# Attention sums kept with heads on partitions, key 0 added by TensorE, division moved to the feed-forward stage

## What is computed

```python
x = x + attn(layernorm(x))
x = x + ffn(layernorm(x))

# attn: attend = |i - j| <= 128, or i == 0, or j == 0
weights = softmax(where(attend, q @ k.T * 0.25, -inf))
out = (weights @ v) @ Wo.T
# ffn: h = x @ ternary(w_fc).T + gate * (x @ v.T @ fast_b.T @ u.T)
#      ternary(relu(h)**2 @ w_proj)
```

## Time and profile before

| | |
|---|---|
| three timed runs | 1067.39, 1068.22, 1068.65 us; median 1068.22 |
| the profiled execution's own time | 1071.5 us |
| its span in the trace | 1068.9 us |
| TensorE busy | 1031.5 us (97%) |
| VectorE busy | 921.4 us (86%) |
| ScalarE busy | 775.2 us (73%) |
| GpSimd busy | 699.6 us (65%) |
| granted TensorE clock | 0.995 of full speed |

### The profile page before, as it was taken

One profiled execution on the slowest core, in us unless ns is written; L12 is line 12 of the kernel. 1 busy time (PEld: TensorE's weight loads), 2 busy tenths in 40 slices (PEclk: granted clock), 3 DMA queues, 4 the chain that ended last, 5 costly groups with the idle time before them and its releaser, 6 DMA issues.

```text
span 1068.9 us, 40083 instructions
## 1 busy us (share of the span) xinstructions
PE 1031.5 (97%) x16071; PEld 789.2 (74%) x16071; DVE 921.4 (86%) x3202; ACT 775.2 (73%) x1328; POOL 699.6 (65%) x945
## 2 busy tenths in 40 slices
PE   9999999799999999999999999999999999999997
PEld 8888887466665666557665666588888888888886
DVE  7889987799999999999999999487888888888885
ACT  7989987687888888887888878854566554556554
POOL 3575556688888888898888888843344443344443
PEclk9999999899999999999999999999999999999999
DMA  6999989878667766776677653512122221123001
GB/s 210 263 314 276 286 231 267 155 136 154 129 139 156 157 126 137 158 145 130 139 138 160 131 120 70 143 38 80 59 89 90 60 60 60 60 79 95 26 21 40
DMA packets 187019, 142.33 MB, mean 133 GB/s; under 512 B 61625, under 2 KB 186577, under 8 KB 186833
## 3 DMA queue, kind: packets, MB, share of 16 engines
q1 hardware_dynamic: 186832, 139.77, 55.3%
HBM read 87.98 MB, written 50.95 MB: 130 GB/s over the span
## 4 chain that ended last, share of the span: by engine, by line
PE 60%; DVE 11%; issue 4%; SPq 3%; ACT 2%; DMA 1%; POOL 0%; DVEq 0%; ACTq 0%
PE e_psum L1616 13%; PE e_psum L1638 12%; PE e_psum L1347 9%; PE e_psum L1906 6%; PE e_psum L1908 6%; DVE a_masked L1362 4%; PE e_psum L1888 3%; PE e_psum L1887 3%; DVE n_stats L144 2%; DVE f_x L2028 2%; SPq L1321 2%; PE e_psum L231 1%; PE e_psum L233 1%; PE e_psum L232 1%; PE e_psum L1892 1%
## 5 line engine op out<-in xcount | busy, mean ns | idle before, releaser
L1692 ACT ACTIVATE a_weights<-e_psum 128x1024 f32<-128x1024 f32 (+1 forms) x512 | 391.4, 809 | 85.2 <-PE e_psum L1616 84.7
L1362 DVE CUSTOM_DVE_ANT_0 a_masked<-e_psum,band 128x290 f32<-128x290 f32 (+1 forms) x992 | 387.7, 445 | 37.9 <-PE e_psum L1347 32.1
L1526 POOL TENSOR_SCALAR_AFFINE_SELECT a_weights<-a_weights 128x1024 f32<-128x1024 f32 x256 | 273.9, 1094 | 48.6 <-ACT a_weights L1692 47.2
L1950 POOL TENSOR_TENSOR f_square<-f_relu 128x512 f32<-128x512 f32 x128 | 147.6, 1154 | 212.8 <-ACT f_relu L1939 189.6
L1347 PE MATMUL e_psum<-e_k,e_q 96*32 96x290 bf16 (+2 forms) x4096 | 236.5, 287 | 15.6 <-DVE max L1362 6.5
L1616 PE MATMUL e_psum<-e_q,e_k 128*32 128x384 bf16 (+2 forms) x5632 | 241.6, 280 | 5.8 <-ACT a_weights L1692 3.6
L1638 PE MATMUL e_psum<-a_weights,a_v 128*17 128x384 f32 (+2 forms) x2816 | 221.7, 389 | 2.0 <-issue 1.4
L1616 PEld LDWEIGHTS e_psum<-e_q,e_k 128*32 128x32 bf16 x5632 | 132.0, 96 | 97.0 <-ACT a_weights L1692 40.9
L1347 PEld LDWEIGHTS e_psum<-e_k,e_q 96*32 96x32 bf16 x4096 | 116.8, 97 | 84.1 <-DVE max L1362 46.7
L1906 PE MATMUL e_psum<-w_w_t,f_square_hi 128*128 128x256 f32 x512 | 129.4, 287 | 4.6 <-DVE f_square_lo L2004 4.6
L1939 ACT ACTIVATE f_relu<-e_psum,w_mag 128x512 f32<-128x512 f32 x128 | 87.4, 683 | 54.5 <-PE e_psum L1892 54.5
(11 more groups left out here) (215 smaller groups left out, 1925.3 us busy)
## 6 DMA issues: line engine op xcount, KB each, us to landing
k_parts<-p_k_parts SPq DMA_DIRECT2D x48, 258.0 KB, 4.7
q_parts<-p_q_parts SPq DMA_DIRECT2D x48, 256.0 KB, 5.5
e_q<-q_parts SPq DMA_DIRECT2D x64, 192.0 KB, 4.0
e_k<-k_parts SPq DMA_DIRECT2D x60, 193.5 KB, 3.7
v_ones<-p_va SPq DMA_DIRECT2D x16, 544.0 KB, 5.9
p_x<-in_x SPq DMA_DIRECT2D x16, 512.0 KB, 7.0
e_q<-q_parts SPq DMA_DIRECT2D x64, 128.0 KB, 3.9
f_o<-attention SPq DMA_DIRECT2D x16, 512.0 KB, 4.7
```

The source lines that it names most:

```text
L1362: dve.tensor_tensor_reduce(out=masked[:, place + lo:place + hi], in0=bank[:, lo:hi], in1=self.band[:, lo:hi], scale=1.0, scalar=NEG, op0=A ...
L1526: pool.affine_select(out=blocks, in_=blocks, compare_op=ALU.is_ge, fill=0.0, base=0, pattern=[[0, NQ // 2 * HEAD_COLS // P // CUT_STEP], [ ...
L1692: act.activation(pe_w[:, us.upar, lo:hi], score[c % 2][:], ACT.Exp).then_inc(s_exp, 1)
L1950: pool.tensor_tensor(sh.r2[:, j % 4, :], sh.r[:, j % 4, :], sh.r[:, j % 4, :], ALU.mult).then_inc(self.s_sq, 1)
```

## The change

What it does, part by part:

- **Sums.** VectorE copies the sums out of PSUM as they are, heads on partitions (`dve_sums_copied`), and SyncE stores each unit's 128 rows of 512 float32 in DRAM, now laid out as [group, head, channel or denominator, token]. The transposition, the reciprocal and four of GpSimd's operations in each unit are gone.
- **Key 0.** ScalarE's weights `p0` of two units are turned by VectorE (128 by 32 elements, once in two units), brought by a DMA onto one partition of each head's quarter (`p0_row`), and TensorE adds them: four matmuls in each unit (`key0_sums`), one for each head, with one contraction row, 17 columns of weights and 512 moving columns, all float32. They start the accumulation, so they come ahead of the blocks. Head j takes row 32j of the array and columns 32j on. The value row of key 0 is kept on every partition. The gate that excludes key 0 for queries whose window has it is now an addition ahead of the exponential.
- **Shift.** The two copies of the split in three move from ScalarE to GpSimd.
- **TensorE's order.** `AFTER_TILE` is written anew, and `BEFORE_TILES` is empty.
- **Division.** In unit 50's step the denominators of the first three sequences are loaded as a tile of 128 by 768, VectorE takes one reciprocal over it in the next step, and it is stored again; the last sequence's 128 by 256 follow in the feed-forward stage (step of group 5). For each group, 16 heads' factors are then loaded and repeated over 16 partitions each, and GpSimd multiplies them into the loaded sums, two operations of 128 by 512 a group (`pool_combine`).
- **Feed-forward.** As channels already stand on partitions, `pe_turn_o` is gone; the split reads SBUF, one group earlier than before. The first half of `pe_attention` moves to where the transpositions were, the second stays behind `pe_output` of the sixth part. The last sum of unit 63 is done in two pairs of heads, as before, now with two key 0 matmuls ahead of each pair.

The diff, cut to its core:

```diff
-P0_BUFS = 2 * UPG
+P0_BUFS = UPG
+SUM_BUFS = 3
...
+ROW0_STORED, FACTORS, COMBINED = 9, 50, (55, UNITS - 2, UNITS - 1)
+LAST_DEN = 4
...
-BEFORE_TILES = (("score", 0), ("score", 1))
+BEFORE_TILES = ()
 AFTER_TILE = (
-    (), (("score", 2),), (), (), (("score", 3), ("score", 4), ("score", 5)),
-    (), (), (("sum", 0),), (("score", 6), ("score", 7), ("sum", 1)),
...
+    (), (), (("score", 0), ("score", 1)), (("score", 2),), (), (("key0", 0), ("score", 3), ("score", 4)), (),
+    (), (), (("score", 5), ("sum", 0)), (("score", 6), ("score", 7)), (), (("sum", 1),),
...
+    def dve_factor(self, dve, first, last):
+        den = self.den_of(first, last)
+        dve.wait_ge(self.s_den, DMA * last)
+        dve.reciprocal(den, den).then_inc(self.s_factor, 1)
...
+    def dve_sums_copied(self, dve, u):
         dve.wait_ge(self.s_sum, u.n + 1)
...
+        wait(dve, self.s_out[u.n % SUM_BUFS], u.n // SUM_BUFS * DMA)
+        dve.tensor_copy(self.sums[:, u.n % SUM_BUFS], self.sum_bank).then_inc(self.s_copied, 1)
+
+    def dve_p0_turned(self, dve, u):
...
+        dve.transpose(self.p0_t[:, u.ppar], self.p0[:, u.p0 - 1:u.p0 + 1].rearrange("p a b -> p (a b)")
+                      ).then_inc(self.s_p0t, 1)
...
+                if (u := at(L_P0)) and u.last:
+                    sp.wait_ge(s_p0t, u.pair + 1)
+                    wait(sp, s_sum, u.n - 3)
+                    sp.dma_start(sh.p0_row[0:P:SUB, u.ppar].rearrange("a u (j r) -> a (u j) r", r=SUB),
+                                 sh.p0_t[:, u.ppar]).then_inc(sh.s_p0row[u.ppar], DMA)
+                if u := at(L_OUT):
+                    first = 1 if u.gi == 0 else 0
+                    sp.wait_ge(s_copied, u.n + 1)
+                    sp.dma_start(o_dram[u.g].rearrange("(a q) e t -> a q e t", q=UPG)[:, u.hq, :, first:GT],
+                                 sums[:, u.n % SUM_BUFS, first:GT]).then_inc(s_out[u.n % SUM_BUFS], DMA)
...
+                if us and us.n in COMBINED:
+                    for k in range(KT):
+                        feed.pool_combine(pool, Group(COMBINED.index(us.n)), k)
...
+                def key0_sums(heads=range(NQ)):
...
+                    pe.wait_ge(sh.s_p0row[up.ppar], (up.phalf + 1) * DMA)
...
+                    wait(pe, s_copied, up.n)
+                    for j in heads:
+                        h = j * UPG + up.hq
+                        pe.matmul(sum_bank[32 * j:32 * j + VW, :], sh.v0[32 * j:32 * j + 1, up.batch % 2, h * VW:h * VW + VW],
+                                  sh.p0_row[32 * j:32 * j + 1, up.ppar, up.upar, :], start=True, stop=False,
+                                  skip_group_check=True)
...
+                if us and us.n == FACTORS + 1:
+                    sh.dve_factor(dve, 0, B - 1)
...
+    def pool_combine(self, pool, q, k):
+        pool.wait_ge(self.s_oin[q.par], (q.half + 1) * KT * DMA)
+        pool.wait_ge(self.s_fin_in, (q.g + 1) * KT * DMA)
+        pool.tensor_tensor(self.sh.o_t[q.par][:, k], self.sh.o_t[q.par][:, k], self.sh.factor[:, k], ALU.mult
+                           ).then_inc(self.s_comb, 1)
...
             if qa:
-                feed.pe_turn_o(pe, qa, qf)
+                feed.pe_attention(pe, qa, (0,))
...
             if qa:
-                feed.pe_attention(pe, qa)
+                feed.pe_attention(pe, qa, (1,))
```

More of the change, by code:

```diff
@@ L2118, in body @@
                     norm.root(act, qx)
[L2119 to L2120 removed]
+                if j in (4, 5) and qn:
+                    feed.act_o_high(act, qn, (j - 4,))
             if qx:
```

416 lines of the change are left out of this document (206 added, 210 removed).

## The result

The changed kernel is slower by more than forecast: **1159.3 us** (median of 4 runs, 1155.9 to 1163.5) against 1068.4 us of the kernel before (4 runs), a ratio of 1.085 with a 95% interval of 1.081 to 1.089. Forecast were 1092 us and a range that ended at 1122. The profiled execution has a span of 1154.2 us against 1068.9, so 85.3 us are to be found.

The account below looks back on a forecast made before the run. Attention was taken as nearly balanced between four engines, feed-forward as bound by TensorE; 35 + 4 + 1.7 + 1 - 17.5 = +24 us gave a median of 1092 us, range 1070 to 1122.

Parts of the forecast that it names:

- Part 1: Attention units: key 0's four matmuls on TensorE make a unit 8.3 us, 0.57 more, over 61 units +35 us.
- 6.97 us of other work: Attention units: TensorE's mean work in a unit of the kernel before, leaving 0.76 us of the 7.73 as slack.
- the wait: Attention units: TensorE waits 0.2 to 0.3 us at its sixth tile for VectorE's read of the second tile.
- relief: Attention units: GpSimd loses four operations and VectorE the reciprocal of 0.25 us, so they have more room.
- Rivals A and B: Attention units: A, slack is filled, +7 instead of +35, chance 0.11; B, nothing is hidden, +65, chance 0.13.
- Part 2: Reciprocals on VectorE: 768 columns in one unit +4 us; the last sequence's 256 in a feed-forward step +1.7.
- Part 3: End of attention: transpositions and a VectorE wait go, key 0 insertions come, +1 us (-2 to +4).
- Part 4: Feed-forward: transpositions and the wait ahead of the first output go, 1.25 us in each of 14 steps, -17.5 us.
- beside slack: Feed-forward: GpSimd's two products a step fall beside its slack, as it is busy for 148 of 369 us.
- SyncE's stores and loads I cost at nothing; their cover is a unit of 8 us: Added DMA stores and loads: no cost, as a unit of 8 us covers them.
- Rival D: Units 61 to 63: the detour through DRAM is late, a stall of some 10 us, 1102 us, chance 0.08.

Follow-up runs that it names:

- the mended one: Changed kernel with products on VectorE except group 3's, x for group 1 loaded earlier, reciprocal later in six pieces, first loads spread, group 0's product earlier: 1110.7 us.
- runs 8 and 9: Changed kernel with its single waits mended, 1123.3 us; then also group 3's product back on GpSimd and group 0's one unit earlier, 1110.7 us.
- run 4: Changed kernel with the products by the reciprocals on VectorE, behind its last operation of each feed-forward step, instead of on GpSimd: 1140.9 us.
- run 5: Kernel before the change with TensorE's output 0 moved behind the ternary layer of tile 4 instead of tile 3: 1072.9 us against 1070.2.

## Why the prediction was wrong, point by point

- **Part 1, +35: measured +37 (0.61 us a unit instead of 0.57), and in the changed kernel the sum adds up.** 6.97 us of other work, 0.98 for the group and 0.36 of waiting make 8.31, where the unit is 8.34 and TensorE idles for 0.9%. Two small errors cancel in it: the group is 0.09 cheaper than 0.87 + 0.2, and the wait is some 0.1 longer than I took. What the runs show besides is that +0.57 isn't the net price that I took it for, 1.07 for key 0 less the slack that relief gives back. By my sum a unit without key 0 is 7.2 us; it is 7.86. Waits for other engines, 0.13 us above the unit of before, take over as soon as TensorE's work shrinks; half of key 0 hides in them, and the relief gave nothing back by itself. That 8.3 came out in spite of this is partly luck: for a quarter of the columns the same sum gives 6.97 + 0.22 + 0.2 + 0.25 = 7.6 us, and 7.86 was measured. Rivals A and B are both out: 8.34 is neither 7.84 nor 8.8.
- **Part 2, +4 and +1.7: the operation was sized well, the wait ahead of it not at all.** 4.95 us for 768 columns (5.4 estimated), but +11.2 us on the path beside the 0.6 of every unit: 8.54 of idle, and behind it seven microseconds at a mean granted clock of 0.60 (638 to 645 us), which costs 2.8 us by estimate (7 x 0.4) and is the rest. I bounded the cost by the operation's length and didn't follow the order store, landing, load, reciprocal on SyncE. One unit later and in pieces, the same reciprocals cost 3 x 0.3 us. The last sequence's, 256 columns, cost 0.4 us in the changed kernel, where the step had another bound, and 1.6 in the mended one, where the estimate of 1.7 is met.
- **Part 3, +1: measured +5.7, of which 1.2 is part 1's.** The last four distances between copies sum to 36.4 us, where before has 29.9; behind the last copy 0.8 us are gained. No run separated this stretch; the mended kernel keeps +4.2 of it. Its cause stays open.
- **Part 4, -17.5: the step that failed is "beside slack", by 23 us.** The stage missed its forecast by 33 us; 23 of them are in the 12 steps behind the first (+9.8 instead of -13.3), and the other 10 in the first step (+8.7 instead of -1.25), which is a matter of transfers (see below). TensorE's gain was right: 21.60 us in the step without products, 1.46 under before, and 21.82 in the mended kernel's steps, which is 1.25 under it. "GpSimd's two products a step are beside slack" was wrong. GpSimd had that slack, but its reads of SBUF take VectorE's away. The prediction priced squares that come up to 0.5 us later, a gain of 0.5 instead of 1.25 a step, and not this mechanism, though the trace of before held it already. Of VectorE's operations on 128x4 elements one lasts 0.80 us there, to 871.68, and the next one 0.16, and GpSimd's square ends at 871.66:

```profile
870.46 1.20 POOL L1950 TENSOR_TENSOR f_square<-f_relu 128x512 f32<-128x512 f32 x1 [0.92 <-ACT f_relu L1939]
```
```profile
870.88 0.80 DVE L167 TENSOR_TENSOR n_newton<-n_var_eps,n_rstd_first 128x4 f32<-128x4 f32 x1
871.71 0.16 DVE L169 TENSOR_TENSOR n_newton<-n_newton,n_rstd_first 128x4 f32<-128x4 f32 x1
```

- **"SyncE's stores and loads I cost at nothing; their cover is a unit of 8 us": wrong by 24 us.** 4.2 at the start, 7.8 and 3.4 in units (beside the 0.6 of each), 8.7 in the first feed-forward step. So it weighs as much as the products do. The 7.8 went when the loads were spread over units (runs 8 and 9); the causes of the other three are read from TensorE's idle times in the trace, and no run took any of them away whole. A unit covers a transfer only if it is issued when its data are ready, and SyncE issues in order: behind 1 MB of other loads, and behind stores that wait for copies. Rival D had named the detour through DRAM, with some 10 us and a chance of 0.08, but laid it at the products of units 61 to 63. It came at the row of weights and at x.
- **Direction.** Slower was given 0.86 and came. The range ended at 1122 since each part had bounds of its own and none held a mechanism that hits several queues together.

## What to carry to other kernels

Before you move work to the engine with the most slack, look at what it reads: in these runs a two-operand operation from SBUF on GpSimd lengthened VectorE's two-operand operations, and its TENSOR_SCALAR on 128x4 too, to its own end, and two extra operations on the busier VectorE were the cheaper place (0.2 against 2.25 us a step), as long as they don't stand ahead of something urgent and wait for a DMA themselves (5.25 us in the first step of run 4). Of each DMA that a change adds, cost the wait of its first user by SyncE's order, what it queues behind and what queues behind it, and not by its bytes. When a mend removes a wait, name the next transfer in line before counting the gain: here the first feed-forward step fell from 31.8 only to 29.2 us.

## What the runs showed that I hadn't expected

- Four float32 matmuls of one row each, on four different row and column blocks of the array, into one PSUM bank, run side by side: 0.98 us for 4 x 512 columns, 0.34 for 4 x 128. The change of the array's division costs some 0.1 us of it.
- VectorE operations of 128x4 elements last 0.8 to 1.2 us beside GpSimd's two-operand work (0.16 alone); MEMSETs of 0.53 us on GpSimd at the same place leave the pair of square_lo at 1.28 us, but a TENSOR_SCALAR of 0.17 us lasts 1.40 beside one.
- 16 KB in small pieces, issued behind about 1 MB, reach their reader 8 us after the issue, against a median of 2.4 us for the small rows of the shift, and TensorE starts behind the idle of 5.34 us at the lower clock: a record of 1.90 us for a group that has 1.05.
- A wait on TensorE that is covered by reordering may come back one engine on, and longer: 0.53 us for ScalarE in place of 0.31 for VectorE (run 5).
